# First attention's outputs kept on chip for its projection, and the next layer's ternary matrices prepared during its last group

## What is computed

```
# layer 0, attention: 16 heads of 16, causal
ctx = softmax(mask(Q K^T) / sqrt(16)) V        # per head, 1024 x 1024
x   = x + (ctx @ Wp.T + bp) + ffn0(xn)         # the sum is kept in acc_d, in HBM

# layer 1, feed-forward: ternary matrices, w1 and w2 (704, 256), w3 (256, 704)
gamma = mean(abs(w))
wq    = clip(round(w / (gamma + 1e-8)), -1, 1) # one gamma per matrix
out   = (sigmoid(xn @ wq1.T) * (xn @ wq2.T)) @ wq3.T
```

## Time and profile before

| | |
|---|---|
| median of three runs | 1561.44 us (1554.37 to 1564.23) |
| profiled execution, time and span | 1554.53 us, 1552.9 us |
| busy, TensorE / VectorE / ScalarE / GpSimd | 79% / 58% / 48% / 33% of the span |
| first attention, seven steady groups and the last | about 220 to 526 us |
| stage "ww" | 530.5 to 625.3 us |
| DMA of `ot`, out and back | 16 stores of 256 KB; 8 loads of 512 KB |

### The profile page before, as it was taken

How to read it: one execution, slowest core, us unless ns; L and a number is a source line. 1 busy time by engine, 2 the same in 40 slices (tenths; PEclk the granted TensorE clock), 3 DMA queues, 4 the chain that set the end, 5 groups by cost and what they waited for, 6 DMA issues and landing times. The chain is left out here.

```text
span 1552.9 us, 22609 instructions
## 1 busy us (share of the span) xinstructions
PE 1229.9 (79%) x7428; PEld 880.5 (57%) x7428; DVE 893.3 (58%) x2331; ACT 742.3 (48%) x1684; POOL 508.9 (33%) x540
## 2 busy tenths in 40 slices
PE   2674819999999468484999999987484999999977
PEld 2574715444444156473677777666373666777656
DVE  7655618888886144344666666740344666666640
ACT  1543502676667304434666666640334666666540
POOL 0121332344331100220555555520221555555520
PEclk9796855899999778787999999998797999999998
DMA  2313267676550294102001011005102001010005
GB/s 81 112 55 111 82 81 65 64 76 77 71 64 17 88 303 135 35 28 85 24 28 49 28 43 34 14 28 156 44 28 85 24 28 49 27 49 28 14 28 163
DMA packets 133158, 101.03 MB, mean 65 GB/s; under 512 B 48240, under 2 KB 120368, under 8 KB 132784
## 3 DMA queue, kind: packets, MB, share of 16 engines
q1 hardware_dynamic: 132000, 98.53, 28.1%
q10 hardware_dynamic: 1040, 1.05, 0.2%
HBM read 56.30 MB, written 34.87 MB: 59 GB/s over the span
## 5 line engine op out<-in xcount | busy, mean ns | idle before, releaser
L748 POOL TENSOR_SCALAR a_p<-a_p,a_rl 128x128 f32<-128x128 f32 (+7 forms) x256 | 214.8, 839 | 403.5 <-DVE a_rl L690 403.4
L731 ACT ACTIVATE a_p<-psum,a_nm 128x128 f32<-128x128 f32 (+7 forms) x256 | 189.3, 739 | 107.7 <-DVE a_nm L684 107.2
L1215 ACT ACTIVATE a_pt<-psum 128x512 f32<-128x512 f32 (+3 forms) x384 | 166.2, 493 | 94.8 <-PE psum L1088 93.6
L781 PE MATMUL psum<-ident,a_p 128*128 128x128 f32 x1152 | 171.1, 276 | 31.6 <-DVE a_pt L717 28.4
L1078 PE MATMUL psum<-a_op_k,a_op_q 64*128 64x512 f32 (+3 forms) x384 | 146.9, 460 | 49.5 <-POOL a_op_k L1024 31.3
L781 PEld LDWEIGHTS psum<-ident,a_p 128*128 128x128 f32 x1152 | 130.3, 141 | 53.6 <-issue 48.4
L803 PE MATMUL psum<-a_pt,v 128*64 128x256 f32 (+1 forms) x1280 | 159.6, 371 | 1.1 <-ACT a_ot L817 1.1
L684 DVE CUSTOM_DVE_ANT_0 psum<-psum,mask_a 128x128 f32<-128x128 f32 (+3 forms) x128 | 63.8, 499 | 149.4 <-PE psum L766 149.3
L715 ACT ACTIVATE a_pt<-psum 128x256 f32<-128x256 f32 (+2 forms) x192 | 87.2, 454 | 96.2 <-PE psum L781 95.2
L1078 PEld LDWEIGHTS psum<-a_op_k,a_op_q 64*128 64x128 f32 x384 | 71.9, 206 | 87.0 <-DVE a_nm L1167 36.6
L717 DVE COPY a_pt<-psum 128x512 f32<-128x512 f32 (+1 forms) x192 | 113.7, 592 | 10.3 <-PE psum L781 8.3
(11 more groups left out here) (257 smaller groups left out, 2805.4 us busy)
## 6 DMA issues: line engine op xcount, KB each, us to landing
a_swap<-a_raw SPq DMA_DIRECT2D x64, 128.0 KB, 2.3
ot_d<-a_ot SPq DMA_DIRECT2D x16, 512.0 KB, 2.6
o_ot<-ot_d SPq DMA_DIRECT2D x16, 512.0 KB, 6.4
a_raw_q<-qk_d SPq DMA_DIRECT2D x48, 128.0 KB, 5.1
a_raw_k<-qk_d SPq DMA_DIRECT2D x48, 128.0 KB, 9.1
a_wf<-wf_d SPq DMA_DIRECT2D x16, 384.0 KB, 3.3
qk_d<-p_stage_h SPq DMA_DIRECT2D x8, 512.0 KB, 2.7
qk_d<-p_stage_l SPq DMA_DIRECT2D x8, 512.0 KB, 3.4
```

What stands on the lines that cost most here:

```text
L731: e.activation(s.p[:, t % NPB, 0:(i + 1) * P], C.score[t % 2][:, 0:(i + 1) * P], ACT.Exp, scale=-1.0, bias=s.nm[:, k:k + 1], accum_out=s.l ...
L748: e.tensor_scalar(s.p[:, t % NPB, 0:(i + 1) * P], s.p[:, t % NPB, 0:(i + 1) * P], s.rl[:, k:k + 1], 1.0, ALU.mult, ALU.mult).then_inc(s.no ...
L781: ins = e.transpose(C.turn[par][:, (k - k0) * P:(k - k0 + 1) * P], s.p[:, tt % NPB, k * P:(k + 1) * P], C.ident[:, :])
L1215: e.activation(pt[:, k // G0 % NPT, hd, off:HALF], bank_b("score", g, k)[:, off:HALF], ACT.Exp, scale=-1.0).then_inc(exped, 1)
```

## The change

`ot` becomes one tile in SBUF for all eight groups (`ot0`). `normalise` writes into it, `output0` reads it there. The 16 stores, the 8 loads and the wait for the stores go.

The tiles of the layer-1 matrices are allocated around the attention. GpSimd zeroes them behind the masks of group 0. SyncE loads `lat` in group 1 and one of the three ternary matrices in each of groups 2, 3 and 4, in the place where the store of the half before stood. In group 7 VectorE sums the magnitudes in slots 1, 3 and 5, TensorE adds them over the partitions in slot 16, and VectorE makes the limits in slot 20 and rounds in slots 20, 23 and 48 (the first of the extra iteration). The three passes of the rounding become two. In the stage "ww" only the loads of `acc_d` and of `fuse1`, the projection, the transposes and the fusing are left. The attention's stage has 34 semaphores to clear, where it had 28; "ww" has 30, where it had 39.

```diff
+LAST = NG0 - 1
+MAGNITUDES = {(LAST, 1): 0, (LAST, 3): 1, (LAST, 5): 2}
+TOTALS = (LAST, 16)
+LIMITS = (LAST, 20)
+TERNARY = {(LAST, 20): 0, (LAST, 23): 1, (LAST + 1, 0): 2}
...
-        ot = ph.sb("ot", [P, NCH, HALF])
+        weights = Ternary(ph, N, sources, raw[0][:, :, :].rearrange("p j t -> p (j t)")[:, 0:HT1 * E])
+        weights.ones = C.ones[:, :]
...
-                def store(g, c):
-                    e.wait_ge(normed, 2 * g + c + 1)
-                    e.dma_start(ot_d[g][:, c * HALF:(c + 1) * HALF], ot[:, c, :]).then_inc(ot_out[c], 16)
...
-                    if g:
-                        store(g - 1, 1)
+                    if g == 1:
+                        weights.load_lat(e)
+                    if 2 <= g < 5:
+                        weights.load(e, g - 2)
                     if g + 1 < NG0:
                         maxima(g + 1, 0)
-                    store(g, 0)
-                store(NG0 - 1, 1)
-                for c in range(NCH):
-                    e.wait_ge(ot_out[c], 16 * NG0)
+                weights.landed(e)
...
+                    if g == 0:
+                        weights.pad(e)
...
+                        if (g, t) == TOTALS:
+                            free_a("totals", g, t)
+                            weights.total(e, bank_a("totals", g, t))
...
-                    wait(e, ot_out[c], 16 * g)
-                    e.tensor_tensor(ot[:, c, :], oraw[:, c, :], bank_a("back", g, c)[:, :], ALU.mult).then_inc(normed, 1)
+                    e.tensor_tensor(ot[:, g, c * HALF:(c + 1) * HALF], oraw[:, c, :], bank_a("back", g, c)[:, :], ALU.mult).then_inc(normed, 1)
...
+                        if (g, t) in MAGNITUDES:
+                            weights.magnitude(e, MAGNITUDES[g, t])
+                        if (g, t) == LIMITS:
+                            weights.limits(e, bank_a("totals", *TOTALS))
+                        if (g, t) in TERNARY:
+                            if TERNARY[g, t] == 0:
+                                e.wait_ge(ordered, 2 * NG0)
+                            weights.ternary(e, TERNARY[g, t])
...
-            e.dma_start(ot[:, :, t], heads[:, :, t]).then_inc(came[n], 16)
-            if tt % 2 == 0:
-                e.wait_ge(came[tt // 2], 32)
-            e.wait_ge(came[tt // 2], 32)
+            e.wait_ge(came[tt // 2], 16)
...
+    def pad(self, e):
+        for m in self.mats:
+            e.memset(m[:, :, :], 0.0).then_inc(self.padded, 1)
+
+    def load_lat(self, e):
+        e.dma_start(self.lat[:, 0, :], self.wq_a[0:P, :]).then_inc(self.lat_in, 16)
+        e.dma_start(self.lat[0:QL - P, 1, :], self.wq_a[P:QL, :]).then_inc(self.lat_in, 16)
+        e.dma_start(self.lat[QL - P:P, 1, :], self.wkv_a[0:KL, :]).then_inc(self.lat_in, 16)
+        e.dma_start(self.lat[0:ROPE, 2, :], self.wkv_a[KL:KL + ROPE, :]).then_inc(self.lat_in, 16)
+
+    def load(self, e, m):
+        full = HID1 // P
+        rest = HID1 - full * P
+        e.wait_ge(self.padded, m + 1)
+        dst, s = self.mats[m], self.came[m]
+        if m == 2:
+            e.dma_start(dst[:, :, 0:HID1], self.w3.rearrange("(m p) e -> p m e", p=P)).then_inc(s, 16)
+            return
+        src = (self.w1, self.w2)[m]
+        e.dma_start(dst[:, 0:full, :], src[0:full * P, :].rearrange("(m p) e -> p m e", p=P)).then_inc(s, 16)
+        e.dma_start(dst[0:rest, full, :], src[full * P:HID1, :]).then_inc(s, 16)
+
+    def landed(self, e):
+        e.wait_ge(self.lat_in, 64)
+
+    def magnitude(self, e, m):
+        e.wait_ge(self.came[m], 32 if m < 2 else 16)
+        e.tensor_reduce(self.part[:, m:m + 1], self.flat[m], AX.X, ALU.add, apply_absolute_value=True).then_inc(self.parts, 1)
+
+    def total(self, e, bank):
+        e.wait_ge(self.parts, 3)
+        e.matmul(bank[:, 0:3], self.ones, self.part[:, :], start=True, stop=True).then_inc(self.totals, 1)
+
+    def limits(self, e, bank):
+        self.link = chained(e, self.step)
+        e.wait_ge(self.totals, 1)
+        self.link(e.tensor_scalar(self.limit[:, :], bank[:, 0:3], 1.0 / (HID1 * E), Q1_EPS, ALU.mult, ALU.add))
+        self.link(e.tensor_scalar(self.limit[:, :], self.limit[:, :], 0.5, None, ALU.mult))
+
+    def ternary(self, e, m):
+        w, lim = self.flat[m], self.limit[:, m:m + 1]
+        self.link(e.tensor_scalar(self.neg, w, -1.0, lim, ALU.mult, ALU.is_gt))
+        self.link(e.scalar_tensor_tensor(out=w, in0=w, scalar=lim, in1=self.neg, op0=ALU.is_gt, op1=ALU.subtract))
...
-            link(e.tensor_scalar(neg[:, :], flat[m], -1.0, limit[:, m:m + 1], ALU.mult, ALU.is_gt))
-            link(e.tensor_scalar(flat[m], flat[m], limit[:, m:m + 1], None, ALU.is_gt))
-            link(e.tensor_tensor(flat[m], flat[m], neg[:, :], ALU.subtract))
-            e.sem_inc(ready_q, 1)
...
+            with ExitStack() as both:
+                def wsb(name, shape, dt=F32):
+                    return both.enter_context(nc.sbuf_tensor(name, shape, dt))
+
+                N = Named()
+                N.lat = wsb("lat", [P, 3, E])
+                N.mats = [wsb("w1n", [P, HT1, E]), wsb("w2n", [P, HT1, E]), wsb("w3n", [P, KE, HT1 * P])]
+                ot = wsb("ot0", [P, NG0, T])
+                attend0(nc, C, qk_d, v_d, ot, m_d, N, (wq_a, wkv_a, w1, w2, w3))
+                with Phase(nc, "ww") as ph:
+                    outputs = [output0(ph.part(f"o0b{b}"), C, w_p, b, ot, acc_d) for b in range(B)]
+                    turn = turn_weights1(ph.part("w1"), C, W, N, [free for _, rest in outputs for free in rest.psum_free])
+                    load, fuse = fuse1(ph.part("fu"), C, W, turn, q_ln, wq_b, wkv_b, wo, wf_d)
+                    run(nc, outputs[0][0], outputs[1][0], load, outputs[0][1], outputs[1][1], turn, fuse)
```

More of the change, by code:

```diff
@@ L133, in pe_transposes @@
     for u, (srcs, _, lo) in enumerate(units):
-        e.wait_ge(*ready[u])
+        if ready:
+            e.wait_ge(*ready[u])
         if u >= len(banks):
@@ L1058, in free_a @@
                             e.wait_ge(inverted, 2 * g + n + 1)
+                        elif kind == "totals":
+                            e.wait_ge(weights.step, 1)
                         else:
@@ L1249, in _, with output0 @@
                             exponential(g, t)
-def output0(ph, C, w_p, b, ot_d, acc_d, before):
+def output0(ph, C, w_p, b, ot_all, acc_d):
     NG = H0 // G0
     x = ph.sb("x", [P, NT, E])
-    ot = ph.sb("ot", [P, NG, T])
+    ot = ot_all[:, b * NG:(b + 1) * NG, :]
     came = [ph.sem(f"came{i}") for i in range(NT // 2)]
@@ L1317, in weights1, with turn_weights1 @@
+def turn_weights1(ph, C, W, N, before):
     turned, high, low = ph.sem("turned"), ph.sem("high"), ph.sem("low")
     banks = C.banks[0:6]
-    full = HID1 // P
-    rest = HID1 - full * P
+    lat, mats = N.lat, N.mats
     units = [([lat[:, i, kt * P:(kt + 1) * P] for i in range(2)],
@@ L1373, in weights1 @@
-    made = Programs(sync=sync, gpsimd=gpsimd, tensor=tensor, vector=vector)
-    made.psum_free = [(ready_q, 3)]
-    def turn(before):
-        def tensor(e):
-            for sem, value in before:
-                e.wait_ge(sem, value)
-            pe_transposes(e, banks, C.ident, units, ready, turned, high, low)
-        def scalar(e):
-            act_high(e, banks, units, turned, high)
-        def vector(e):
-            dve_low(e, banks, units, high, low)
-        made = Programs(tensor=tensor, scalar=scalar, vector=vector)
-        made.psum_free = [(high, len(units)), (low, n_lat)]
-        return made
@@ L1392, in weights1, with scalar @@
-    made.turn = turn
+    def tensor(e):
+        for sem, value in before:
+            e.wait_ge(sem, value)
+        pe_transposes(e, banks, C.ident, units, None, turned, high, low)
+    def scalar(e):
+        act_high(e, banks, units, turned, high)
+    def vector(e):
+        dve_low(e, banks, units, high, low)
+    made = Programs(tensor=tensor, scalar=scalar, vector=vector)
+    made.psum_free = [(high, len(units)), (low, n_lat)]
     return made
@@ L2036, in program @@
             W.wof = lsb("w_of", [P, NG1, E])
-            with Phase(nc, "ww") as ph:
-                w = weights1(ph.part("w1"), C, W, wq_a, wkv_a, w1, w2, w3)
-                outputs = [output0(ph.part(f"o0b{b}"), C, w_p, b, ot_d, acc_d, w.psum_free) for b in range(B)]
-                turn = w.turn([free for _, rest in outputs for free in rest.psum_free])
-                load, fuse = fuse1(ph.part("fu"), C, W, turn, q_ln, wq_b, wkv_b, wo, wf_d)
-                run(nc, w, outputs[0][0], outputs[1][0], load, outputs[0][1], outputs[1][1], turn, fuse)
+            with ExitStack() as both:
[11 more added lines that the diff above has]
+                    run(nc, outputs[0][0], outputs[1][0], load, outputs[0][1], outputs[1][1], turn, fuse)
             with nc.Fori(0, B) as b:
```

57 lines of the change are left out of this document (13 added, 44 removed).

## The result

The changed kernel took 1533.28 us (median of 5, 1530.07 to 1547.14); the kernel before, run beside it, 1558.57 (5 runs, 1554.03 to 1564.23). The ratio is 0.9863, 95% interval 0.9831 to 0.9895; in a second comparison on another chip it was 0.9851 (0.9826 to 0.9877). So 21 to 23 us are gained of the 29.9 that my rows gave (32 against the median of the first three runs); by more than 1% it is faster, as forecast.

What follows compares the result with a forecast made beforehand. The prediction saw a 33.4 us hole between attention and projection as the bound; 29.3 + 0.6 = 29.9 us off 1554.5 gave 1524.6, plus 4 to 5 for the profiled execution being fast: 1529 us, range 1519 to 1541.

Steps and rivals of the forecast that it cites:

- the hole in front of the projection: Between attention's last operation and projection's first matmul, 33.4 us in which stores, loads, sums and roundings follow one another.
- the part on the attention: What the work moved into the attention costs there, in four places: together 1.2 us, bounds 0 and 7.6.
- two of my own signs: Projection's first matmul at 529 to 531 was expected; the last group's end moving over 3 us would mean failure.
- What goes: Between attention and projection: without delay in the attention, the projection starts at 528.7, right after the barrier, instead of 559.16.
- Step (a): Between groups 0 and 1, GpSimd zeroes three tiles in 4.1 us; cost taken as 0.5 us, bounds 0 and 1.8.
- step (d): Attention's tail: rounding the third matrix delays GpSimd's last mask; 0.3 us taken, bounds 0 and 2.4.
- Steps (b) and (c): Last group: sums and partition matmul cost 0.2 us each; limits and rounding two matrices cost 0, bounds 0 and 2.3.
- SyncE: In the attention, matrix loads ahead of the row maxima's trip add 1.3 plus some 0.5 us; 3.1 in hand, cost 0.
- the third rival: Row maxima get stuck behind matrix loads in SyncE's queue: 1535, or 1573 at the slower end; chance 0.07, of which 0.02 slower.
- the first: Behind the projection, the fusing waits for its inputs, landing 10.1 us late: 1539; chance 0.05.
- the second: In the last group, the 14.1 us of sums and rounding isn't covered: 1543 in full, a quarter expected at most; chance 0.08.
- The sum: Whole kernel: 29.3 us from the earlier projection plus 0.6 from fewer clears, 29.9 us off the profiled 1554.5.

Runs made afterwards that it cites:

- the clears moved: The changed kernel with the three tiles zeroed at the start of the attention's stage instead of between groups 0 and 1: 1522.98 us, ratio 0.9812 against the kernel before.
- outputs alone: Against the kernel before, only the attention's outputs stay on chip; matrices are loaded, summed and rounded after the attention as before: 1552.52 us, ratio 1.0002.
- matrices alone: Against the kernel before, only the matrices are loaded, summed and rounded in the attention; `ot` still goes by way of HBM: 1539.15 us, ratio 0.9913.
- the second execution of the change: Profiled execution, 1536.82 us, from timing the unaltered changed kernel again on another chip; median there 1530.44 us, ratio 0.9851 against the kernel before.

## Why the prediction was right, and where its size was off

The verdict and the case held: faster, by the hole in front of the projection, with 1533.28 inside the range. But two of my own signs came out against the part on the attention: the projection's first matmul came at 549.35 and 537.50 and not at 529 to 531, and the end of the last group moved by 20.6 and 8.7 us where I had called more than 3 a failure. The median still lies in the range because that had room for other things, the scatter of the runs and two rivals that did not come, and the missed cost fitted into it; this much is luck. By its steps:

- *What goes.* Right to 0.1 us. I had 2.9 us from the last multiplication to the projection (525.8 to 528.7); all traces of the whole change show 2.97 or 2.98. The low clock at the projection's start was there, and the projection took 29.7 us in the profiled executions of before and after (29.5 to 30.8 in the other kernels whose projection starts at the barrier).
- *Step (a), zeroing between the groups*, taken at 0.5 us with bounds of 0 and 1.8. **This is the mis-sized term: it is 7 to 10 us** by the traces (244.8 and 247.7 against 237.4), 6 by the ratios with the clears moved and 7.5 by the medians. I followed the delay along GpSimd's own order, to the next mask and its product, and that was right as far as it went: the mask that stood at 299.7 in my working had room. I did not ask what VectorE does beside those 4.1 us. It had a copy between two SBUF tiles to make, which the clears hold up; row maxima queue behind it, TensorE behind those, and then the clock falls, which makes 4 to 12 us out of 1.9 to 3.6 us of waiting (4.2, 8.8 and 11.7 over 236.0). I had used the Trainium skill's rule (page "SBUF — State Buffer", section "SBUF: two separate sides") for VectorE's passes shutting out GpSimd's masks in step (d) alone. The same section gives the exclusive lock for the other way too, to whichever of the two starts first and for its whole instruction, and names casts among the operations that can need it. The row of 3.50 us agrees with it, and so do the ends of the stretched casts, 0.02 to 0.03 us behind the end of a clear.
- *Steps (b) and (c).* Together 0.4 taken. All added work of the last group costs about 0.7 at like clocks, of which 0.4 or more is the third rounding, so at most about 0.3 is left for these. The pass over two tensors took 1.82 us for the 1.76 I chose over 2.78.
- *Step (d)*, 0.3 taken: 0.4 to 0.9 measured, where I had worked out 0.1 to 0.7 by the Trainium skill's rule (page and section as in step (a)); the rows of 0.77 and 1.08 us agree with that rule, and the tail without these passes has 0.64.
- *SyncE.* The trip of the maxima held, with less in hand than I said. From the first load's issue to the return's it took 370.37 - 363.54 = 6.8 us; in the earlier trace rows from the store's 354.53 - 350.39 = 4.1. That is 2.7 more, where I had expected 1.8 and counted 3.1 in hand. Rows of after, group 2:

```profile
363.54 2.17 SPq L1348 DMA_DIRECT2D w1n<-in_L_ffn_w_dram  x1
365.75 0.54 SPq L1349 DMA_DIRECT2D w1n<-in_L_ffn_w_dram  x1
366.39 0.52 SPq L995 DMA_DIRECT2D m_d<-a_mt  x1
370.37 1.27 SPq L1001 DMA_DIRECT2D a_op_q<-m_d  x2
```

  Steady groups took 33.3 us with the loads and without, so the third rival did not come. Neither did the first (no DMA before the fusing) nor the second (0.7 us and not 14).
- *The sum.* My 29.9, with the attention's 1.2 taken off, is the gain of the kernel with the clears moved (29.2 us by its ratio, 0.9812). With (a) at 7 instead of 0.5 my working gives 1529 + 6.5 = 1535.5, within 3 us of the median. What I added for the profiled execution being the fast one (4 to 5 us) fits the 1558.57 that stood beside the change, 4.0 above the profiled 1554.53 (three of its five runs are the three I had), but not the 1553.77 and 1554.13 on two other chips.

## What to carry to other kernels

Work put on an idle engine must be held against what *every other* engine does in those microseconds, not only against that engine's next duty: look on the time line for short operations between SBUF tiles that stand under the new work and have a queue behind them. A wait of TensorE in a dense stretch costs more than its length once the clock falls behind it, so split or shrink such fillers (here to the columns that need them) or place them where nothing dense follows. Where two conditions stand before one instruction, taking away the one that is met first shows little or nothing: with the clears in their first place outputs alone gained 0, matrices alone 14 us, both 23, and 29 once the clears were out of the way.

## What the runs showed of the hardware that was not expected

GpSimd's clears (writes only, 1.38 us for 128x1536) hold a VectorE copy of 128x16 until one of them ends: 0.86, 2.18 or 3.50 us for 0.17. Whether it gets in between two clears queued back to back differs from one execution to the next (behind the second in two, behind the third in one). VectorE's maxima out of PSUM were not stretched beside the clears that stood between the masks (two of them 1.36 us with and without). In the tail it goes both ways: the third rounding's second pass took 2.07 us beside a mask for 1.82.

TensorE's granted clock held at 1.00 behind one wait of 0.61 us and fell to 0.50 behind waits of 1.92, 1.93 and 3.62; how long it stayed there, with TensorE busy nearly throughout, was not the same for the same wait: about 20 us at 0.50 in the second execution of the change, about 7 in matrices alone, whose waits were 1.93 and 1.92. What sets that length no run here shows. Two short waits close together, 0.66 and 0.56 us, were followed by the low clock in 3 executions of 12, at 7 us each. And the clock also fell without any such wait: in the kernel before it was 0.50 from 376 to 378, with no wait of TensorE over 0.3 us since 366, and that group took 1 us longer.
